# A convolution kernel on one core: the first pair of images is stored as 112 partitions without their tails and sixteen partitions whole

## The reference

```python
def _gn(v, G=16, eps=1e-5):                     # two channels make a group
    g = v.reshape(B_, G, C_ // G, H_, W_)
    m = mean(g, axis=(2, 3, 4)); s = var(g, axis=(2, 3, 4))
    return ((g - m) / sqrt(s + eps)).reshape(v.shape)

x = x + conv(_gn(x), weight, bias)              # by FFT of size 256, cropped
```

## Time and profile before

| | us |
|---|---|
| median of 3 runs | 82.92 (82.86 to 83.15) |
| the profiled execution | 82.75 |
| its span, from the first to the last instruction | 81.5 |
| TensorE busy in the span | 67.7 |
| VectorE busy | 50.2 |
| ScalarE busy | 48.0 |
| GpSimd busy | 31.6 |
| bytes moved | 33.62 MB |

### The profile page before, as it was taken

How to read it: one execution, slowest core, us unless ns; L and a number is a source line. 1 busy time by engine, 2 the same in 40 slices (tenths; PEclk the granted TensorE clock), 3 DMA queues, 4 the chain that set the end, 5 groups by cost and what they waited for, 6 DMA issues and landing times.

```text
span 81.5 us, 684 instructions
## 1 busy us (share of the span) xinstructions
PE 67.7 (83%) x222; PEld 41.8 (51%) x222; DVE 50.2 (62%) x43; ACT 48.0 (59%) x53; POOL 31.6 (39%) x43
## 2 busy tenths in 40 slices
PE   0019865999999999999999999999999999999000
PEld 0014424556666666666666666666666665665000
DVE  0019936960399779949994996899499735100700
ACT  3308958980299669947974994799299553000000
POOL 6994000004029950000999690086029206800000
PEclk9999995557999999999999999999999999999998
DMA  1999999999979997799597997979969999988976
GB/s 21 336 434 438 458 426 408 457 461 466 482 338 466 399 608 336 336 608 399 238 546 337 490 490 279 529 305 514 498 289 466 418 402 466 480 382 382 525 325 253
DMA packets 2020, 33.62 MB, mean 412 GB/s; under 512 B 280, under 2 KB 314, under 8 KB 484
## 3 DMA queue, kind: packets, MB, share of 16 engines
q1 hardware_dynamic: 1876, 33.36, 96.1%
q0 software_dynamic: 96, 0.19, 0.7%
q10 hardware_dynamic: 48, 0.06, 0.3%
HBM read 16.84 MB, written 16.78 MB: 412 GB/s over the span
## 4 chain that ended last, share of the span: by engine, by line
PE 77%; DMA 14%; DVE 2%; SPq 1%; issue 0%; POOL 0%; POOLq 0%
PE ps L437 75%; DMA images<-x_dram 14%; DVE images L453 2%; PE ps_m L339 1%; SPq L195 1%; PE ps_w L285 1%; POOL pair L233 0%; POOL eps L199 0%; POOLq L605 0%
## 5 line engine op out<-in xcount | busy, mean ns | idle before, releaser
L437 PE MATMUL ps<-g,w_sb 128*128 128x363 f32 (+1 forms) x192 | 61.9, 480 | 0.0
L437 PEld LDWEIGHTS ps<-g,w_sb 128*128 128x128 f32 x192 | 36.6, 197 | 20.5 <-issue 2.3
L418 POOL TENSOR_SCALAR images<-images,bias_sb 128x1984 f32<-128x1984 f32 (+3 forms) x12 | 23.2, 1941 | 26.9 <-ACT origin L313 18.4
L303 DVE TENSOR_REDUCE sums<-images 128x1 f32<-128x4096 f32 x7 | 30.9, 4411 | 0.6 <-DMA images<-x_dram 0.6
L324 ACT ACTIVATE unused<-images,origin 128x4096 f32<-128x4096 f32 (+1 forms) x9 | 30.0, 3331 | 0.3
L453 DVE SCALAR_TENSOR_TENSOR images<-ps,bias_sb,images 128x1089 f32<-128x1089 f32 (+2 forms) x9 | 10.9, 1221 | 7.7 <-PE ps L437 7.7
L394 ACT ACTIVATE g<-images,rstd 128x1089 f32<-128x1089 f32 (+2 forms) x8 | 9.4, 1192 | 3.4 <-DVE rstd L368 3.4
L303 DVE TENSOR_REDUCE first_sums<-images 128x1 f32<-128x2048 f32 x2 | 4.6, 2286 | 5.9 <-DMA images<-x_dram 5.9
L356 DVE TENSOR_SCALAR var<-ps_m,square 128x1 f32<-128x1 f32 x8 | 1.7, 218 | 9.4 <-ACT square L351 9.4
L351 ACT ACTIVATE square<-ps_m,origin 128x1 f32<-128x1 f32 x8 | 2.1, 262 | 8.4 <-PE ps_m L339 8.4
L285 PE MATMUL ps_w<-images,avg 128*128 128x1 f32 x4 | 1.1, 355 | 6.9 <-POOL bias_sb L499 5.9
(11 more groups left out here) (21 smaller groups left out, 13.0 us busy)
## 6 DMA issues: line engine op xcount, KB each, us to landing
images<-x_dram SPq DMA_DIRECT2D x1, 5344.0 KB, 36.8
images<-x_dram SPq DMA_DIRECT2D x1, 4096.0 KB, 24.6
out_dram<-images SPq DMA_DIRECT2D x1, 4096.0 KB
out_dram<-images SPq DMA_DIRECT2D x2, 2048.0 KB
out_dram<-images SPq DMA_DIRECT2D x1, 3904.0 KB
out_dram<-images SPq DMA_DIRECT2D x1, 3040.0 KB
images<-x_dram SPq DMA_DIRECT2D x1, 2080.0 KB, 15.5
images<-x_dram SPq DMA_DIRECT2D x2, 1024.0 KB, 5.8
```

Of the source, the lines that this page charges most:

```text
L303: lambda e: e.tensor_reduce(to_sum(img, k)[:, 0:1], piece, mybir.AxisListType.X, ALU.add),
L418: "pool", lambda e: e.tensor_scalar(part, part, 1.0, bias_sb, op0=ALU.mult, op1=ALU.add),
L437: lambda e, k=k, dc=dc, rows=rows, top=top: e.matmul(ps[:, 0:rows, 0 : N - dc], w_sb[:, k * P : (k + 1) * P], g[:, top : top + rows, dc:N] ...
```

## The change

`MOST` becomes 112. SyncE's first store of pair 0 covers the first `most` numbers of partitions 0 to 111 alone; its second store, which held the tails of two partitions, now holds sixteen partitions, 112 to 127, whole (32 KB each). GpSimd stores the tails of 112 partitions; in its output order eight tails lie one behind the other, where it was three. The host's reordering follows. Semaphores, waits and the order of the instructions stay.

```diff
-    MOST = 126
+    MOST = 112
@@ in the loop over the images
             if img == 2:
-                store(flat(out[0])[:, :most], flat(pairs[0])[:, :most], begin, *finished(0, 1))
-                store(flat(out[0])[MOST:P, most:], flat(pairs[0])[MOST:P, most:], *finished(0, 1))
+                store(flat(out[0])[0:MOST, :most], flat(pairs[0])[0:MOST, :most], begin, *finished(0, 1))
+                store(out[0, MOST:P], pairs[0][MOST:P], *finished(0, 1))
@@
                 if img == 2:
-                    spread = flat(out[0])[0:MOST, most:].rearrange("(b a) n -> a b n", b=3)
+                    spread = flat(out[0])[0:MOST, most:].rearrange("(b a) n -> a b n", b=8)
                     moved = store(spread, flat(pairs[0])[0:MOST, most:], *biased[1], turned, by="pool")
@@ on the host
-    last = out[0, :126, 1, -6:]
-    last[:] = last.reshape(3, 42, *last.shape[1:]).transpose(1, 0, 2, 3).reshape(last.shape)
+    last = out[0, :112, 1, -6:]
+    last[:] = last.reshape(8, 14, *last.shape[1:]).transpose(1, 0, 2, 3).reshape(last.shape)
```

## The result

The changed kernel takes 92.26 us (median of 6 runs, 91.49 to 92.48) against 82.93 (82.86 to 83.15): a ratio of 1.1107, with a 95% interval of 1.1066 to 1.1147. Ratios compare fast runs alone, and of all kernels here only the one with its two stores in the other order had slower runs besides. The direction is the one forecast; the size, +9.3 us, is nearly twice the +5.0 of the sum and lies outside the range.

A forecast was written before the change was run, and what follows sets the result against it. The DMA engines, never idle from the first packet on, were taken to bound the kernel. Losses of 3.4 (sixteen partitions) and 1.6 us (the 112) made +5.0, from 82.92 to 87.9 us; forecast 86 to 90.5, range 84.0 to 90.5.

The forecast's parts named there:

- the sum: Pair 0's two SyncE stores: 3.4 for the sixteen partitions plus 1.6 for the 112, +5.0 us, all reaching the end.
- The bound: DMA engines never idle from the first packet on, so work lengthened behind 40 us moves the end by as much.
- What stays: SyncE's seven stores, GpSimd's one DMA instruction and the computation: nil, covered by the work up to 78 us.
- the bytes of each engine: Tails dealt anew: an engine's load changes by -1.5, 0 or +1.5 KB, at most 0.06 us either way.
- The two prices: Slower reading in pair 0's two SyncE stores: +3.4 us for the sixteen whole partitions, +1.6 us for the 112.
- half the weights' rate: Sixteen whole partitions: weights ran at 14.2 GB/s into 32 partitions; halved for half as many, 4.62 us, +3.4.
- the tails' 22.2 GB/s: Store of the 112 partitions, seven to an engine: rate of all tails together before the change, 9.85 us, +1.6.
- What the profile was to show: Chain end unmoved, last wait about 9 us, DMA share near 97%, 388 GB/s, packets stretched between 41 and 55 us.
- No sharing: Rival: every engine moves its 26.6 GB/s from whatever partitions; not slower, 82.9 us; chance 0.11.
- Partial sharing: Rival: ways carry more than one engine's rate, or few engines meet; 84 to 86 us; chance 0.17.
- The heavier case: Rival: runs of seven at the upper end, 93.5 us, or the sixteen on few engines; over 90.5; chance 0.06.

The follow-up runs named there:

- runs of seven alone: Changed kernel, but in place of the sixteen whole partitions, 4 KB from each of 128 partitions goes to a scratch array: 86.86 us.
- sixteen alone: Changed kernel, but pair 0's bulk leaves all 128 partitions, seven eighths of each row, and partitions 112 to 127 go whole to a scratch array: 86.72 us.
- every eighth: As sixteen alone, but the sixteen whole partitions are 0, 8, 16 and so on to 120: 85.01 us.
- every seventh: As sixteen alone, but the sixteen whole partitions are 0, 7, 14 and so on to 105: 85.08 us.
- changed, with the wait: Changed kernel, but SyncE's store of pair 1 also waits until both of its stores of pair 0 have landed: 88.98 us.
- GpSimd's part alone: Kernel before, but GpSimd stores 112 tails by eights and SyncE the sixteen remaining tails; bulk of all 128 partitions in one store: 82.99 us.

## Why the size was wrong

| kernel | mean engine late (us) | span longer (us) |
|---|---|---|
| changed | 5.3 | 9.6 |
| runs of seven alone | 2.0 | 4.0 |
| sixteen alone | 3.4 | 4.0 |
| every eighth | 1.4 | 1.8 |
| every seventh | 0.5 | 2.5 |
| changed, with the wait | 6.3, idle time within | 6.3 |

The first column is worked out from the share of the last window as above for each; a packet that straddles the window's start makes it uncertain by some 0.4 us. The second is the profiled execution's.

**The bound: right.** The engines have no idle time up to 78 us, the chain ends where it did, and the loss went into SyncE's last wait.

**What stays, and the bytes of each engine: right.** GpSimd's part alone is 0.1 to 0.2 us off the kernel before, near the 0.06 us forecast.

**The two prices: right, as means.** The sixteen were put at half the weights' rate, 7.1 GB/s, a loss of 3.4; alone they run at 7.0 GB/s and the mean engine is 3.4 late. The runs of seven were put at the tails' 22.2 GB/s, a loss of 1.6; they run at 21.9 and the mean engine is 2.0 late. The sum, +5.0, is close to the lateness of the mean engine, 5.3. Part of this is luck. The prices were carried over from rows of other shapes, and the weights' row, as the prediction says itself, is one of small packets, whose slowness no run here takes apart. And in the changed kernel the sixteen lost their 3.4 us in another way than alone, as the part on how the prices depend on each other shows below. The mechanism for the sixteen, partitions that share their ways out of the memory, is shown by the three kernels that differ in the source of sixteen rows alone. That the runs of seven are slow for the same reason is argued and not shown. The Trainium skill, page SBUF — State Buffer, section Door 1: The DMA port swizzle, gives four ports for sixteen neighbours and 104 GB/s; the sixteen packets of 32 KB at 4.7 us are 112 GB/s, so the trace agrees within a tenth. By the same section of the Trainium skill every eighth partition reaches eight ports, and the packets there, 2.2 us in the mean, less than half of 4.7, fit that.

**The step that failed** is the sentence behind the sum: "All of it lies on the engines behind 40.5 us, where they don't idle, and so at the end". The kernel ends with its last engine, and the rates that went into the sum are means over engines. Nothing behind the two stores makes up for an engine that is late. By the packet records the last packet of pair 1 starts at 60.4 us before, at 64.5 with the runs of seven alone, 64.2 with the sixteen alone and 70.1 in the changed kernel: 4.1, 3.8 and 9.7 us late already there, and 4.0, 4.0 and 9.6 at the end, while the other engines finish and stand. For the runs of seven this step doubles the price, from 2.0 to 4.0 us; for the sixteen, which meet in step, it adds 0.6.

**And the two prices were not independent.** 4.05 and 3.9 make 7.95; the change costs 9.3. The runs of seven spread the engines: by the packet records the sixteen packets start between 50.7 and 53.4 us, alone between 50.0 and 50.9. (The records don't name the engine of a packet. The sixteen are taken to be those that start where a packet of the bulk, or a tail behind it, ends; of two that start at 52.46 us the longer is taken for one of them.) Engines that are through early go on to pair 1, and beside it the sixteen take 1.2 to 8.8 us, 4.6 in the mean (4.2 if the shorter of the two is taken). With the wait they start as far apart but without pair 1 beside them, and take 1.2 to 4.4 us, 2.85 in the mean; the last one ends at 56.7 us instead of 61.6. So it is pair 1's packets that hold up some of the sixteen. Without them the spread would have made the sixteen cheaper, a loss of some 1.6 us on the mean engine and not 3.4.

Kept away from pair 1 by the wait, the two stores cost 88.98 - 82.79 = 6.2 us, of which the wait itself is some 1.1 if it costs here what it does beside the sixteen. How the share among those who meet is settled is open. Pair 1's own packets of the time were stretched to 2.4 us at most by the same reading, so the longest of the sixteen got less than an even part. Coming late is not by itself what makes a packet slow: of the sixteen the three longest start at 52.5 to 52.8 us, but the two that start last, at 53.4, take 2.4 and 2.7. Which partitions a run of seven gives to which engine wasn't tried.

**What the profile was to show.** A wait of about 9 us at the end was 14.2; 388 GB/s was 369; a DMA share near 97% is 92.1 + 0.6 + 0.3 = 93%, and this was the sign to look for: idle engines at the end mean uneven ones. The packets stretched where and about as far as said: 1.42 us in the mean for 31.2 KB (some 1.4), while of the sixteen one kept 1.2 and three took over 8 (4 to 5). The last of them ends at 61.6 us, where the extra was to lie before 55.

**The rivals.** No sharing is out. Partial sharing is out as a forecast, though its condition, engines so spread that few meet, did arise (2.85 us with the wait); pair 1's packets undid the gain. The heavier case, put over 90.5, is where the time lies, but not by its mechanism: the runs of seven did not fall to 14.2 GB/s, and the sixteen did go over all engines.

No kernel here beats the one before; the tails alone come within 0.2%.

## What to carry to other kernels

A DMA queue that is never idle ends with its slowest engine: when a change makes some packets slow, ask which engine gets them and whether anything behind evens it out, and price the slowest, not the mean; a share that falls off in the last slices of the profile is its mark. Keep transfers that must run at full rate on all 128 partitions, and cut them along the row; here sixteen neighbouring partitions gave a quarter of the rate. Before two disturbances are added, ask whether the first changes how the engines meet in the second.

## What was not expected of the hardware

A wait in front of a store made a kernel bound by its DMA engines faster, 92.3 to 89.0 us, because it kept pair 1's packets from slowing the sixteen (their mean fell from 4.6 to 2.85 us); where the engines were level the same wait cost 1.06 us. A packet of 32 KB that took 1.21 us elsewhere took 8.8 us beside the next store, 3.7 GB/s, about half of the 7.0 GB/s that the sixteen had in step.
